# A transformer layer on one core: a new order and new pieces for the prologue

## The reference

```
x = x + LN(Attention(LN(x)))
x = x + LN(FFN(LN(x)))

Attention: q, k, v = LN(x) @ Wq + bq, ... @ Wk + bk, ... @ Wv + bv     (2 heads of 64)
  the upper 32 of each head's 64 columns of q and k are turned by rotary angles:
  base = sigmoid(nrope_freq) * 3400 + 8300;  freq_i = base ** (-i/16), i = 0..15
  angle(p, i) = p * freq_i * 2 pi / 255,  p = 0..255
  softmax(q k^T / 8) v, then @ Wo + bo
FFN: x @ W^T, plus one of four low-rank products (ranks 1, 2, 4, 8), picked per row by a
  softmax over normalised router logits (Wp, bp, sim, temp)
```

## Time and profile before

| what | before |
|---|---|
| median of the runs | 164.67 us |
| profiled execution: time of that run | 165.49 us |
| profiled execution: span, first to last instruction | 163.7 us |
| busy share PE / DVE / ACT / POOL | 81 / 78 / 68 / 55% |
| mean granted TensorE clock | 0.917 |

### The profile page before, as it was taken

One profiled execution on the slowest core, in us unless ns is written; L12 is line 12 of the kernel. 1 busy time (PEld: TensorE's weight loads), 2 busy tenths in 40 slices (PEclk: granted clock), 3 DMA queues, 4 the chain that ended last, 5 costly groups with the idle time before them and its releaser, 6 DMA issues.

```text
span 163.7 us, 3006 instructions
## 1 busy us (share of the span) xinstructions
PE 132.5 (81%) x865; PEld 106.9 (65%) x865; DVE 128.4 (78%) x540; ACT 111.2 (68%) x369; POOL 89.8 (55%) x148
## 2 busy tenths in 40 slices
PE   0467579988989999999999999999999699166040
PEld 0246257877779778887987888798788589135010
DVE  3569966586798999999989998898797798754602
ACT  3157545883979699789969997996997767240130
POOL 4281960580566595867767685875569506405201
PEclk9999956999999999999999999999999999955555
DMA  3524230000000000200020010001001000001001
GB/s 100 185 72 122 70 122 0 4 2 0 2 0 4 2 0 0 68 0 0 2 68 2 0 64 4 0 0 64 2 6 64 0 4 34 30 0 64 0 0 64
DMA packets 4911, 5.02 MB, mean 31 GB/s; under 512 B 369, under 2 KB 4640, under 8 KB 4896
## 3 DMA queue, kind: packets, MB, share of 16 engines
q1 hardware_dynamic: 4512, 4.46, 8.5%
q10 hardware_dynamic: 384, 0.38, 0.7%
HBM read 2.74 MB, written 2.10 MB: 30 GB/s over the span
## 4 chain that ended last, share of the span: by engine, by line
PE 71%; DVE 13%; ACT 6%; POOL 3%; DMA 3%; issue 2%; POOLq 1%; DVEq 0%; ACTq 0%
PE ps_s L838 11%; PE ps_a L858 8%; PE ps_z L879 7%; PE ps_b L858 5%; PE ps_c L858 4%; PE ps_a L848 4%; PE ps_z L892 4%; PE ps_b L812 3%; DMA x_all<-x 3%; PE ps_b L848 3%; PE ps_c L828 2%; PE ps_s L869 2%; PE ps_c L848 2%; PE ps_s L828 2%; PE ps_d L819 2%
## 5 line engine op out<-in xcount | busy, mean ns | idle before, releaser
L320 ACT ACTIVATE probs<-ps_s,neg_max 128x256 f32<-128x256 f32 x64 | 27.1, 489 | 11.8 <-DVE neg_max L474 11.8
L474 DVE TENSOR_REDUCE neg_max<-ps_s 128x2 f32<-128x512 f32 x32 | 21.7, 683 | 4.6 <-PE ps_s L838 4.6
L838 PE MATMUL ps_s<-qk_t 64*128 64x256 f32 x128 | 19.2, 418 | 0.9 <-ACT probs L320 0.9
L858 PE MATMUL ps_a<-v_all,probs_t 128*128 128x129 f32 x128 | 17.6, 280 | 0.0
L858 PEld LDWEIGHTS ps_a<-v_all,probs_t 128*128 128x128 f32 x128 | 15.6, 191 | 2.3 <-issue 2.3
L216 POOL TENSOR_TENSOR turn<-qk,sin_x 128x256 f32<-128x256 f32 x16 | 11.7, 733 | 9.4 <-ACT qk L304 9.0
L879 PE MATMUL ps_z<-w_z,x_t 128*128 128x190 f32 x64 | 13.9, 352 | 2.2 <-DVE x_all L589 2.2
L838 PEld LDWEIGHTS ps_s<-qk_t 64*128 64x128 f32 x128 | 11.9, 195 | 5.8 <-issue 5.2
L589 DVE SCALAR_TENSOR_TENSOR x_all<-ps_z,rsz,x_all 128x128 f32<-128x128 f32 x32 | 9.3, 345 | 7.6 <-POOL rsz L237 7.6
L227 POOL TENSOR_TENSOR inv_norm<-norm,power 128x4 f32<-128x4 f32 x8 | 8.1, 1014 | 13.0 <-DVE norm L543 13.0
L231 POOL TENSOR_TENSOR rsy<-var_y,power 128x4 f32<-128x4 f32 x8 | 8.6, 1071 | 11.5 <-ACT sq_y L331 11.5
(11 more groups left out here) (198 smaller groups left out, 403.6 us busy)
## 6 DMA issues: line engine op xcount, KB each, us to landing
x_all<-x SPq DMA_DIRECT2D x8, 256.0 KB, 2.7
out<-x_all SPq DMA_DIRECT2D x7, 256.0 KB, 2.1
vec<-vectors ACTq DMA_DIRECT2D x1, 273.0 KB, 4.3
w_raw<-w_attn SPq DMA_DIRECT2D x1, 256.0 KB, 5.1
out<-x_all SPq DMA_DIRECT2D x2, 128.0 KB, 1.7
ffn_raw<-w_ffn ACTq DMA_DIRECT2D x1, 71.5 KB
down_raw<-w_down ACTq DMA_DIRECT2D x1, 23.5 KB
sim_raw<-sim ACTq DMA_DIRECT2D x1, 0.5 KB
```

The source lines that it names most:

```text
L320: last = act.activation(probs[:, u, j, :], ps_s[u % 2][:, j * T:(j + 1) * T], ACT.Exp, bias=neg_max[:, u, j:j + 1])
L474: dve.tensor_reduce(neg_max[:, u, :], ps_s[u % 2][:, :].rearrange("p (j k) -> p j k", j=TILES), AX.X, ALU.max, negate=True).then_inc(max_r ...
L838: last = pe.matmul(ps_s[h][:, j * T:(j + 1) * T], qk_t[r, b, 0, j * P:(j + 1) * P], qk_t[r, b, 1, :], start=True, stop=True)
L858: last = pe.matmul(unit_bank[u][:, j * VW:(j + 1) * VW], probs_t[:, u, i, j * P:(j + 1) * P], v_all[:, at:at + VW], start=(i == 0), stop=( ...
```

## The change

The change touches the prologue and what of it is moved to pass 0. Passes now start at 0.

- Loads. x of group 0 comes as two DMAs of one sequence each (`xa_loaded`, `xb_loaded`); the weights come as Wq, Wk (issued by ScalarE) and Wv, Wo (issued by SyncE). The vector of all biases is no longer broadcast to 128 partitions in one load. In its place are: two scalars on 32 partitions, the q and k bias as one row, bv as one column (`bv_col`, a 4-byte piece on each of 128 partitions), and bo with bp broadcast (`bo_bp`). x of group 1 is issued without a wait; the feed-forward weights come behind it on SyncE's queue.
- Group 0 goes through statistics, normalisation, transposes and projections in two halves (one sequence each). q and k columns come first (`first_qk`, 256 columns a matmul, two tiles in one bank), v columns later (`first_v`).
- The bias of q and k is added by a matmul with one contraction row.
- The angles are a matmul of positions (16 rows) with a diagonal of frequencies. The cosine comes from sin of half the angle: 2 s^2 - 1.
- VectorE does the rotary turn of the first half, and the shift `nm` of groups 0 and 1; ScalarE does the upper parts of the weights and the centring of Wo.
- ScalarE's tables are switched by dummy activations (`spare`) placed ahead of their use.
- `centre_bias`, `rows_low(1)` and the statistics of group 2 stand in pass 0 behind `row_max(0, 1)`. Parts 2 and 3 of `later_weights` change places, and the power for `sim_n` stands earlier on GpSimd.

The new orders, cut to what matters here:

```
# SyncE
+            sp.dma_start(x_all[:, 0:T], x_d[:, 0, :]).then_inc(xa_loaded, 16)
+            sp.dma_start(scal[:, :], vectors[AT_TEMP:AT_TEMP + 2].partition_broadcast(PROJ)).then_inc(scal_loaded, 16)
+            sp.dma_start(x_all[:, T:2 * T], x_d[:, 1, :]).then_inc(xb_loaded, 16)
+            sp.dma_start(w_raw[:, 2 * E:4 * E], w_attn[:, 2 * E:4 * E]).then_inc(wvo_loaded, 16)
...
+                if n == 1:
+                    sp.dma_start(bv_col[:, :], vectors[AT_BV:AT_BV + E].rearrange("(p o) -> p o", o=1)).then_inc(late_loaded, 16)
+                    sp.dma_start(bo_bp[:, :], vectors[AT_BO:AT_BO + E + PROJ].partition_broadcast(P)).then_inc(late_loaded, 16)
...
# GpSimd
+            pool.wait_ge(base_ready, 1)
+            pool.tensor_tensor(freq_c[:, 3:4], freq_c[:, 2:3], expo[:, :], ALU.pow).then_inc(inv_ready, 1)
+            for k in range(2):
+                pool.wait_ge(var0, k + 1)
+                pool.tensor_tensor(rs1[:, 0, half(k)], ve1[:, 0, half(k)], power[:, half(k)], ALU.pow).then_inc(rstd0, 1)
+            pool.wait_ge(late_loaded, 32)
+            pool.tensor_copy(bv_wide[:, :], bv_col[:, :].to_broadcast([P, P])).then_inc(bv_ready, 1)
+            norm_rows(1)
+            rope(0, 1)
# ScalarE, ahead of pass 0
+            act.activation(spare[:, :], eps[:, 0:1], ACT.Sin)
...
+            up_first(0)
...
+            qk_first(0)
+            act.activation(spare[:, :], eps[:, 0:1], ACT.Exp)
+            up_first(1)
...
+            qkt_copy(0, 0)
+            qk_first(1)
+            act.wait_ge(shift1, 1)
+            normalise(1)
# ScalarE, pass 0
                 if now:
                     exps(a, 0)
+                if a == 0:
+                    v_first(0)
+                    rows_up(1)
+                    v_first(1)
# VectorE, ahead of pass 0 (calls; small operations in words)
#   first_stats(0), frequency base, first_variance(0), diagonal, first_stats(1), first_shift(0), xn of half 0,
#   w_low of q and k, angles, first_low(0), first_variance(1), tables, first_shift(1), xn of half 1,
#   rotary turn of half 0, first_low(1), stats(1, 0..3), gap/mean/variance(1), w_low of v, bias_y,
#   later_weights(0), shift of group 1, xn of two tiles of group 1
# VectorE, pass 0, behind row_max(a, 1)
                 if a == 0:
+                    rows_low(1)
+                    centre_bias()
                     later_weights(1)
+                    for t in range(PT):
+                        stats(2, t)
+                    gap(2)
+                    mean(2)
+                    variance(2)
# TensorE, behind the fold of the weights
+            first_turn(1)
+            turn_qk(0, 0, None)
+            first_qk(1)
+            scores(0, 0, None)
+            first_v(0)
+            turn_x(1)
+            first_v(1)
+            later_weights(0)
```

More of the change, by code:

```diff
@@ L275, in _, with up_first, qk_first, v_first @@
         def _(act):
[L276 to L291, removed]
+            act.dma_start(w_raw[:, 0:2 * E], w_attn[:, 0:2 * E]).then_inc(wqk_loaded, 16)
+            act.dma_start(bias_qk[:, :], vectors[0:2 * E].rearrange("(o c) -> o c", o=1)).then_inc(bias_loaded, 16)
+            act.wait_ge(scal_loaded, 16)
+            act.activation(freq_c[:, 0:1], scal[0:ROT, 1:2], ACT.Exp, scale=-1.0).then_inc(freq_exp, 1)
+            act.wait_ge(heat_in, 1)
+            act.activation(heat[:, 0:1], heat[:, 1:2], ACT.Exp).then_inc(heat_ready, 1)
+            def up_first(k):
+                act.wait_ge(xt0_done, k + 1)
+                act.activation(xn_up0[:, half(k), :].rearrange("p t c -> p (t c)"), xt0_bank[k][:, 0:2 * P], ACT.Copy).then_inc(xt0_out, 1)
+            def qk_first(k):
+                act.wait_ge(qkv_done, k + 1)
+                act.activation(qk[:, half(k), :, :].rearrange("p t g c -> p (t g c)"), qk0_bank[k][:, :], ACT.Copy).then_inc(qk_out, 2)
+            def v_first(k):
+                act.wait_ge(qkv_done, k + 3)
+                if k == 0:
+                    act.wait_ge(pool_consts, 4)
+                at = 2 * k * VT
+                act.activation(v_all[:, at:at + 2 * VT].rearrange("p (h c) -> p h c", c=VW)[:, :, 0:E],
+                               v0_bank[k][:, :].rearrange("p (h c) -> p h c", c=E), ACT.Copy).then_inc(v_out, 2)
             def normalise(n):
@@ new lines, in _ @@
+            first_variance(0)
+            dve.wait_ge(inv_ready, 1)
+            dve.tensor_scalar(freq_d[:, :], ident[0:ROT, 0:ROT], freq_c[:, 3:4], None, ALU.mult).then_inc(diag_ready, 1)
+            first_stats(1)
+            first_shift(0)
+            dve.wait_ge(shift0, 1)
+            for t in (0, 1):
+                last = dve.tensor_scalar(xn[:, t, :], x_all[:, rows(0, t)], rs1[:, 0, t:t + 1], nm1[:, 0, t:t + 1],
+                                         ALU.mult, ALU.add)
+            last.then_inc(xna_ready, 1)
@@ new lines, in _ @@
+            first_shift(1)
+            dve.wait_ge(shift0, 2)
+            for t in (2, 3):
+                last = dve.tensor_scalar(xn[:, t, :], x_all[:, rows(0, t)], rs1[:, 0, t:t + 1], nm1[:, 0, t:t + 1],
+                                         ALU.mult, ALU.add)
+            last.then_inc(xnb_ready, 1)
+            dve.wait_ge(tables_ready, 4)
+            dve.wait_ge(qk_out, 2)
+            spatial = qk[:, 0:2, :, :].rearrange("p t g c -> p (t g) c")[:, :, 2 * ROT:4 * ROT]
+            swapped = spatial.rearrange("p g (h i) -> p g h i", h=2)[:, :, ::-1, :]
@@ L922, in _, with first_turn @@
-            pe.wait_ge(turned_out, 1)
-            pe.wait_ge(fold_link, 3)
-            pe.matmul(ps_z1[:, 0:E], turned[0:HD, 0:P], wo_c[0:HD, :], start=True, stop=True)
-            pe.matmul(ps_z0[:, 0:E], turned[HD:2 * HD, 0:P], wo_c[HD:2 * HD, :], start=True, stop=True)
-            pe.matmul(ps_s0[:, 0:E], turned[:, P:2 * P], wo_c[:, :], start=True, stop=True).then_inc(fold_mm, 1)
-            turn_x(0)
-            pe.wait_ge(front_ready, 1)
+            def first_turn(k):
+                pe.wait_ge(xnb_ready if k else xna_ready, 1)
+                for t in range(2):
+                    last = pe.transpose(xt0_bank[k][:, t * P:(t + 1) * P], xn[:, 2 * k + t, :], ident[:, :])
+                last.then_inc(xt0_done, 1)
@@ new lines, in first_products, with first_qk @@
+            def first_products(bank, k, cols):
+                for t in range(2):
+                    o = bank[:, t * 2 * E:(t + 1) * 2 * E]
+                    pe.matmul(o, xn_low0[:, 2 * k + t, :], w_up[:, cols], start=True, stop=False)
+                    pe.matmul(o, xn_up0[:, 2 * k + t, :], w_up[:, cols], start=False, stop=False)
+                    last = pe.matmul(o, xn_up0[:, 2 * k + t, :], w_low[:, cols], start=False, stop=True)
+                last.then_inc(qkv_done, 1)
+            def first_qk(k):
+                pe.wait_ge(xt0_low, k + 1)
+                pe.wait_ge(wqk_ready, 1)
+                first_products(qk0_bank[k], k, slice(0, 2 * E))
@@ new lines, in _ @@
+            pe.wait_ge(diag_ready, 1)
+            for j in range(TILES):
+                last = pe.matmul(ps_z1[:, j * ROT:(j + 1) * ROT], pos[:, j, :], freq_d[:, :], start=True, stop=True)
+            last.then_inc(angle_mm, 1)
+            first_turn(0)
+            pe.wait_ge(wvo_loaded, 16)
+            pe.matmul(ps_z0[:, 0:P], w_raw[:, 2 * E:3 * E], centre[:, :], start=True, stop=True).then_inc(fold_turn, 1)
+            first_qk(0)
+            pe.wait_ge(turned_out, 1)
+            pe.wait_ge(wo_ready, 1)
@@ L964, in _ @@
                 if nxt:
-                    turn_qk(a + 1, 0, (probs_ready, 4 * a + 4) if now else (xt_low, 1))
+                    turn_qk(a + 1, 0, (probs_ready, 4 * a + 4))
                 if now:
@@ L975, in _ @@
                     project_z(a - 1, 1)
-                if a == -1:
-                    later_weights(0)
                 if nxt:
-                    scores(a + 1, 0, (x2t_out, a) if last_ else (probs_ready, 4 * a + 3) if now else (fold_link, 5))
+                    scores(a + 1, 0, (x2t_out, a) if last_ else (probs_ready, 4 * a + 3))
                 if now:
```

313 lines of the change are left out of this document (182 added, 131 removed).

## The result

The changed kernel takes 159.12 us (median; 159.04 to 159.19), the kernel before 164.94 us beside it. The ratio is 0.9645, 95% interval 0.9607 to 0.9684: 5.8 us faster, forecast 4.4 (160.3 us, range 157.8 to 163.3). The profiled execution after took 159.12 us with a span of 157.3 us; before 165.49 and 163.7. The spans differ by 6.4 us, 0.6 more than the medians: the profiled run before lies that much over its median.

The account below looks back on a forecast made before the run. TensorE sets the pace of unchanged passes, so only their start moves, through a prologue waiting on VectorE. 3.9 + 0.5 = 4.4 us off the span, 163.7 to 159.3; median 160.3 us, range 157.8 to 163.3.

Parts of the forecast that it names:

- The placing of the prologue: Group 0's prologue, timed step by step: first statistics 3.8 us, first scores done 16.1 to 17.1 (old 25.73), 9 us won.
- What is given back: Behind the first scores, waits on VectorE's prologue work: group 1's projection starts at 22.3, only 4.4 to 4.5 us earlier.
- The first part of the sum, 3.9: Pass 0, exponentials of the second pair of units: start at 28.1 against 31.97, 3.9 us won.
- The second part, 0.5: Pass 0, TensorE's 1.09 us wait for `sim_r`: new order removes it, but group 2's late low rows leave 0.5 us won.
- Rival (a), the clock: Half-speed stretch covers 4.5 us more of bound TensorE work in pass 0: 2.2 us lost, 162.5 us; chance 0.20.
- Rival (b), VectorE lighter: Prologue: no xn contention (1.0), loads at 2.9 (0.9), all of 1.09 `sim_r` wait kept: 2.1 us more, 158.2; chance 0.13.
- Rival (c): GpSimd's `bv_col`, `bo_bp` loads land past 10.4, each us late costs one; slower than before from 14.8; chance 0.07.
- (d): Gain given back whole: pass 1 waits for something that does not move, within 0.5% of 164.7 us; chance 0.05.

Follow-up runs that it names:

- Experiments 2: Changed kernel with GpSimd's rotary turn of the second half held until group 1 is normalised: 157.88 us, ratio 0.9568 to the kernel before.
- 3: Changed kernel with row maxima and exponentials of unit 0 moved ahead of group 1's shift and normalisation: 157.76 us, ratio 0.9589 to the kernel before.
- 7: Changed kernel with the loads of bv_col and bo_bp issued behind x of group 3: 161.91 us.
- experiment 1: Changed kernel with the order of later_weights parts 2 and 3 and of GpSimd's power for sim_n put back as before: 160.42 us.
- experiment 9: Kernel before, with unused transposes filling TensorE's prologue idle time and the new order of later_weights parts 2 and 3 and sim_n's power: 161.65 us (0.9792).
- experiment 8: Kernel before, with 8 and 10 unused identity transposes on TensorE around group 0's q, k transposes: 162.91 us, ratio 0.9875.
- experiments 5: Changed kernel with x of group 0 in one 256 KB load, both halves waiting for it: 159.46 us.
- 6: Changed kernel with the old 273 KB broadcast of all vectors loaded again, unused, ahead of Wq, Wk on ScalarE's queue: 160.76 us.
- experiment 12: Changed kernel with unit 0's maxima and exponentials first and unused transposes on TensorE in the drain and the prologue: 156.49 us, ratio 0.9459 to the kernel before.
- 11: Changed kernel with unit 0's maxima and exponentials first and unused transposes where TensorE idles in the drain: 156.19 us, ratio 0.9471 to the kernel before.

## Why the prediction was right, and where it was short

The direction, the place and the mechanism up to the first projection were right. The forecast's sum was 4.4 us; the two profiles differ by 6.5 at the same event, the medians by 5.8.

- *The placing of the prologue.* xn of half 0 was done at 6.94 (predicted 7.35), first statistics began at 3.37 (3.8), VectorE came to group 1's statistics at 13.13 (13.65), to the first maxima at 18.07 (18.8), TensorE to the projection at 21.46 (22.3). Two terms made most of the error. The first load took 2.6 us, not 3.1. The copy in `later_weights(0)` took 0.19, not 0.67: its row before stood beside GpSimd's 128x256 operations, and in the new place only a power of four columns runs on GpSimd (14.74 for 1.01). I read the contention in xn and not in this one.
- *What is given back.* Right as far as the projection: 10 us at the scores become 5.3 there (forecast 4.5), through VectorE's order. Experiments 2 and 3 take 1.0 us each out of this chain, 7 shows that a late piece costs its full delay.
- *The first part of the sum, 3.9.* At its own event, the exponentials of the second pair, it was 5.0 (31.97 to 26.93): 0.8 to 0.9 from the placing, the rest in pass 0, where the maxima came 0.9 behind the scores' end (25.29), not 1.1. But the event was the wrong one. I took the 4.5 of the projection down to 3.9 because VectorE has new work in pass 0 and its maxima come late. They do, and with the new order around `sim_r` it costs nothing: TensorE had other work until these exponentials were there, and its 5.3 us stayed 5.3 (24.23 against 29.53) and 5.4 (30.06 against 35.44) up to the products with `sim_r`.
- *The second part, 0.5.* This term failed. Between the two kernels it is 1.2 (5.38 becomes 6.54); experiment 1 gives 1.55, experiment 9 gives 1.39 on the old kernel. The step "what are late next are the low rows of group 2, 0.5 us earlier than before" was wrong: the wait at `sim_r` came off whole, and the next low rows held nothing up.
- *Rival (a), the clock.* It had the sign wrong. I saw the old half-speed stretch as something that might grow; the changed kernel has no such stretch, and experiment 8 prices the old one at 2.4 us. In the forecast this gain lay hidden in the comparison with old times that hold it, and was named nowhere. That the changed kernel escaped such a stretch was luck: its TensorE idles as I feared (1.66 us ahead of 18.20), and nothing in the forecast says why the clock should stay. Of 6.5 us at the scores of pass 1 about 2.4 are the clock, 1.2 to 1.4 the order around `sim_r`, and 2.8 the shorter prologue (39.97 in experiment 9 to 37.52 is 2.45, and the first statistics of experiment 9 began 0.35 before those of the kernel before, 5.17 against 5.52). The loads of experiments 5 and 6 would be 2.3 of these 2.8. What the halves, the one-row bias matmul, the new angles and the moved work bring by themselves no run shows.
- *Rival (b), VectorE lighter,* came about in part (loads 0.4 earlier, all of the 1.09 kept), with xn still contended: 158.2 was its price, 159.12 the result. Its three parts (1.0, 0.9 and the other 0.6 of the 1.09) add to 2.5, not to the 2.1 I wrote. *Rival (c)* was priced right and absent, *(d)* was absent: pass lengths did not change (scores of passes 2 and 3 at 52.04 and 66.66 in the chain after, 14.62 apart; 14.64 before).

## What to carry to other kernels

A prologue cut by 10 us is worth what is left at the first event that the steady loop waits for; follow the engine whose order stands between, and take the event from the chain: here it was the first projection (5.3), and the maxima behind it (4.4) cost nothing. Read the clock row of both kernels before pricing such a change: two short waits of TensorE ahead of a busy stretch cost 2.4 us here, nearly as much as the shorter prologue brought. And when a small operation shows a long time, look for what streams beside it before carrying that time to a new place.

## What the runs showed of the hardware

Two `tensor_scalar` of 128x128 on VectorE took 0.60 us with GpSimd idle and 1.68 with GpSimd's 128x256 operations beside them. The Trainium skill says as much ("SBUF — State Buffer", "Who interferes with whom": GpSimd and some kinds of VectorE operation share one pair of ports, and whichever comes second waits), and the trace agrees for these operations; which came second it does not show. Beside GpSimd's power of four columns (14.74 for 1.01) the copy at 15.48 took 0.19, against 0.67 beside a 128x256 operation.

The clock's first rise was not where I looked for it. The same code gave scores of 1.13 us at 14.50 (after) and of 1.96 at 14.90 (experiment 1), and 1.91 with a prologue filled from 1.70 on (experiment 12). The profile's clock row reads full speed in all of them there, though 256-column matmuls follow each other at 0.21 us there (9.00, 9.21 after) and at 0.12 later (16.02, 16.14): 1.2 and 2.4 GHz. Fillers kept a clock that was up (experiments 8 and 11); in the one profile with fillers in the new prologue they did not bring it up sooner.

Nor does the length of one wait tell when it falls. TensorE's two waits ahead of the half-speed stretch, before, and its wait after:

```profile
19.56 0.66 PE L828 MATMUL ps_s<-ident,qk 128*128 128x128 f32 x4 [1.19 <-POOL qk L222]
21.56 1.12 PE L812 MATMUL ps_b<-ident,xn 128*128 128x128 f32 x4 [1.34 <-DVE xn L463]
```

```profile
18.20 0.66 PE L920 MATMUL ps_b<-ident,xn 128*128 128x128 f32 x4 [1.66 <-DVE xn L789]
```

Before, the clock fell at 20.3, in the second wait. After, one wait of 1.66 us left it up, and no profile with the new prologue shows a half-speed stretch between the clock's first rise and the drain. What decides between the two is left open.
